# Routing of a mixture-of-experts stage: the slot arithmetic of a batch moved to the head of the next step, its four row transfers issued together

## The chip, the cores and the metric

The kernel runs on one core of a Trainium2 chip. The metric is the device time of one execution in microseconds. Five engines work side by side, each through its own instructions in a fixed order: TensorE (PE; its weight loads are shown as PEld), VectorE (DVE), ScalarE (ACT), GpSimd (POOL) and SyncE (SP, which here only issues transfers). They meet only at semaphores.

## What is computed

32 batches of 256 rows by 256 features go through two layers. The change lies in the first stage, which for each batch does the latent cross-attention of the first layer and the routing for the first feed-forward layer. Cut to what matters:

```python
x = x + tanh(g_xattn[0]) * xattn(ctx, layernorm(x), ...)     # 8 heads of 64, 376 keys
h = layernorm(x)
probs = softmax(h @ Wr + br)                    # 8 experts, for each row
topk_p, topk_e = top_k(probs, 2)
pos = (how many earlier choices of this batch took the same expert)
keep = pos < cap                                # cap = 40 rows of a batch for each expert
flat_idx = (e * B + b) * cap + min(pos, cap - 1)
buf[flat_idx] += h * keep                       # rows sent to their experts
y = relu(buf @ W1[e] + b1[e]) @ W2[e] + b2[e]   # second stage
```

The experts and the second layer follow in later stages, which the change doesn't touch.

## The kernel before

The first stage (`attend`) is a software pipeline of 35 steps, written out one after the other: step `s` begins batch `s`, does most of the attention of batches `s-1` and `s-2`, the output projection and both normalisations of batch `s-3`, and the routing of batches `s-4` and `s-5`. In every engine's `step(s, p)` the calls stand in the order in which that engine executes them; nothing else sets the order. So an instruction that waits holds up all that is written below it on its engine. `q` is `1 - p`, the other half of the double buffers.

For batch b the routing runs as follows.

- `x1_standardise` (ACT, L215) writes the normalised rows `x2h[:, p]`. It waits until the transfers that read this half two batches ago have landed (`sent[p]`), and those are the transfers of the batch whose turn came two steps before.
- `weigh` (POOL, L253) multiplies these rows by one expert's router weights, once for each of 8 experts: eight products of 128x512. `logit_part` (DVE, L259) sums each up. There are four buffers, so product e waits for the sum of product e-4. The last sum, `logit_part(7)`, and `logits_sum`, `logits_shift` and `choose(0)` to `choose(7)` (softmax, the two best experts, their one-hot rows `oh`) stand in the next step.
- `router_count` (PE, L381) counts choices with three small matmuls into the bank `a_work`, and `counts_in` (DVE, L325) takes them out of it.
- `place(0)` to `place(4)` (DVE, L335 to L355) are ten instructions on tiles of 128x4 to 128x32: the first row of each expert's region (`at_b`), two sums, the test against the capacity (`kept`, L342), the slot, the indices `sidx`, the weight (L352) and the row number (L355).
- `dispatch` (POOL, L205) issues four indirect transfers, each of which sends 128 rows of `x2h` to `slots` by a column of `sidx`. It waits for the last instruction of `place`.

The other names that the prediction uses: `row_max` (DVE, L914) takes scores out of PSUM with their row maxima and `exps` (ACT, L769) follows it; `turn_prob` (PE, L1221) transposes the exponentials and `turned_out` copies them out of PSUM, half on ACT (L777) and half on DVE (L934); `v_out` (ACT, L762) frees `a_work`; `turn_c` (PE, L1148) and `router_count` wait for it; `att_low` (DVE, L947) subtracts two tiles in SBUF; `output` (PE) is the output projection and `out_stat` (DVE, L953) its statistics; on POOL `norm1` and `norm2` turn statistics of batch `s-3` into scales, `norm0` (L181 to L190 on `a_var`, `a_nm`, `a_rs`, `a_sh`) those of batch `s`, and `residual` (L669) is an addition of 128x512.

In the kernel before, `place` of batch `s-4` stands in the second half of DVE's step, among `row_max`, `turned_out` and the first sums of the products of batch `s-3`, while GpSimd computes these products. `dispatch` of batch `s-5` is cut in two: two transfers behind `norm1`, two behind `norm2`.

Of the kernel before, what the change touches and what calls it, by code (L numbers as in the profile page):

```python
# [398 lines left out]
def attend(nc, t, keep):  # L399
# [3 lines left out]
    with ctx:  # L403
# [245 lines left out]
        def _(eng):  # L649
# [22 lines left out]
            def step(s, p):  # L672
                q = 1 - p
                if isinstance(s, int) and s == 4:
                    eng.wait_ge(zeroed, 16 * N_CLEAR)
                if here(s - 3):
                    norm1(eng, s - 3)
                if routed(s - 5):
                    dispatch(eng, s - 5, q, range(QT))
                if live(s):  # L680
                    norm0(s)
                if here(s - 3):
                    norm2(eng, s - 3)
                if routed(s - 5):
                    dispatch(eng, s - 5, q, range(QT, QT * 2))
                if live(s - 2):
                    residual(s - 2, p)
                if here(s - 3):
                    for e in range(E0):
                        weigh(eng, s - 3, q, e)  # L690
# [6 lines left out]
        def _(eng):  # L697
# [91 lines left out]
            def step(s, p):  # L789
# [15 lines left out]
                if live(s - 2):  # L805
                    k_high(s - 2, p, 3)
                    exps(s - 2, 5, 0)
                    exps(s - 2, 5, 1)
                if here(s - 4):
                    router_exp(eng, s - 4)  # L810
                if live(s - 2):
                    v_out(s - 2, p, 0)
                    turned_out(s - 2, 2, 0)
# [64 lines left out]
        def _(eng):  # L878
# [101 lines left out]
            def step(s, p):  # L980
# [17 lines left out]
                if live(s - 2):  # L998
                    turned_out(s - 2, 1, 1)
                if here(s - 4):  # L1000
                    logit_part(eng, s - 4, 7)
                if live(s - 2):
                    row_max(s - 2, p, 5, 0)
                if live(s - 3):
                    att_low(s - 3, 3)
                if here(s - 4):
                    logits_sum(eng, s - 4)
                if live(s - 2):
                    row_max(s - 2, p, 5, 1)
                if isinstance(s, int) and s == B + 2:  # L1010
                    w1_lower(1)
                if here(s - 4):
                    logits_shift(eng, s - 4)
                if live(s - 1):
                    mask_line(s - 1, q)
                if live(s - 2):
                    over_sum(s - 2, 1)
                if live(s - 1) and not (isinstance(s, int) and s == 1):
                    kvin_low(s - 1, q, 0)
                if here(s - 4):  # L1020
                    choose(eng, s - 4, 0)
                if live(s - 1) and not (isinstance(s, int) and s == 1):
                    kvin_low(s - 1, q, 1)
                if here(s - 4):
                    choose(eng, s - 4, 1)
                if live(s - 3):
                    out_stat(s - 3)
                if here(s - 4):
                    choose(eng, s - 4, 2)
                if live(s - 2):  # L1030
                    turned_out(s - 2, 2, 1)
                if here(s - 4):
                    choose(eng, s - 4, 3)
                if live(s - 3):
                    out_centre(s - 3)
                if live(s - 2):
                    row_max(s - 2, p, 6, 0)
                if here(s - 4):
                    choose(eng, s - 4, 4)
# [3 lines left out]
                if here(s - 4):  # L1043
                    choose(eng, s - 4, 5)
# [3 lines left out]
                if here(s - 4):  # L1048
                    choose(eng, s - 4, 6)
# [3 lines left out]
                if here(s - 4):  # L1053
                    choose(eng, s - 4, 7)
                if live(s - 2):
                    row_max(s - 2, p, 7, 1)
                if here(s - 3):
                    out_norm(eng, s - 3, q)
                if live(s):
# [26 lines left out]
                if routed(s - 4):  # L1086
                    place(eng, s - 4, p, 0)
                if live(s - 1):
                    row_max(s - 1, q, 2, 1)
                if routed(s - 4):  # L1090
                    place(eng, s - 4, p, 1)
# [4 lines left out]
                if routed(s - 4):  # L1096
                    place(eng, s - 4, p, 2)
# [4 lines left out]
                if routed(s - 4):  # L1102
                    place(eng, s - 4, p, 3)
# [4 lines left out]
                if routed(s - 4):  # L1108
                    place(eng, s - 4, p, 4)
# [1569 lines left out]
```

## Time and profile before

| | us |
|---|---|
| median of 3 runs | 2470.74 (2461.04 to 2481.05) |
| the profiled execution | 2471.47 |
| its span, first to last instruction | 2469.7 |
| first stage, up to about | 1393 |
| of it 26 alike steps, 142.4 to 1232.4 | 1090.0, so 41.92 for each |
| PE busy in these | 942.43 of 1090.0 |
| DVE, ACT, POOL busy in these | 851.52, 631.30, 562.00 |

The span is cut by time: the stretches are bounded by `out_stat`, which opens the second third of a step. All times of rows are of this one execution, in microseconds from its start.

### The profile page before, as it was taken

How to read it: one execution, taken by the hardware profiler on the slowest of the kernel's cores; microseconds unless marked ns; L12 is line 12 of the kernel's file. 1: busy time of each engine (PE TensorE's matmuls, PEld its weight loads, DVE VectorE, ACT ScalarE, POOL GpSimd, SP SyncE). 2: the span in 40 equal slices, each digit the busy share in tenths (PEclk: the TensorE clock that was granted, in tenths of full speed). 3: DMA queues.
4: the chain of work that ended last, by engine and by line, in shares of the span. 5: the costliest groups of instructions: out<-in, count | busy, mean ns of one | idle time of the engine just before them, and what ended most of it. 6: DMA issues, size and time to landing. Idle time of an engine off the chain costs nothing. (4 is left out here: it accounts for less than half of the span.)

```text
span 2469.7 us, 48999 instructions
## 1 busy us (share of the span) xinstructions
PE 2257.1 (91%) x15114; PEld 1860.6 (75%) x15114; DVE 1860.9 (75%) x5977; ACT 1288.7 (52%) x3220; POOL 1021.0 (41%) x1410
## 2 busy tenths in 40 slices
PE   9988888989888888888896999999998999999998
PEld 6756565656565666666664999999997888888886
DVE  5787878778787878777877755555557899899887
ACT  6655655555555565556562433333334555555553
POOL 1445555464645454545455200000025555555541
PEclk9989898999899898899897999999999999999999
DMA  5321111111111111111101422222122222122210
GB/s 202 123 70 33 46 33 38 42 35 44 36 44 35 40 39 40 33 46 41 32 28 56 146 80 91 80 78 78 45 83 58 60 71 63 61 71 63 60 52 18
DMA packets 136370, 147.71 MB, mean 60 GB/s; under 512 B 23106, under 2 KB 122681, under 8 KB 135856
## 3 DMA queue, kind: packets, MB, share of 16 engines
q1 hardware_dynamic: 122969, 123.18, 15.5%
q0 software_dynamic: 12288, 21.21, 3.0%
q8 instruction: 124, 2.03, 0.3%
q14 instruction: 134, 1.10, 0.1%
q10 hardware_dynamic: 855, 0.19, 0.1%
HBM read 102.09 MB, written 54.79 MB: 64 GB/s over the span
## 5 line engine op out<-in xcount | busy, mean ns | idle before, releaser
L769 ACT ACTIVATE a_prob<-a_prob,a_nmax 128x376 f32<-128x376 f32 x512 | 309.2, 605 | 267.3 <-DVE a_nmax L914 265.2
L914 DVE CUSTOM_DVE_ANT_0 a_prob<-a_score,a_mask_row 128x376 f32<-128x376 f32 x512 | 273.6, 541 | 59.1 <-PE a_score L1212 53.6
L1517 ACT ACTIVATE e_hidden<-e_first,keep_b 128x256 f32<-128x256 f32 x320 | 134.6, 472 | 281.2 <-PE e_first L80 279.4
L1212 PE MATMUL a_score<-a_kT,a_qT 64*128 64x376 f32 x1024 | 242.3, 585 | 27.9 <-DVE a_nmax L914 27.9
L1221 PE MATMUL a_turned<-keep_ident,a_prob 128*128 128x128 f32 (+1 forms) x1536 | 229.2, 286 | 27.7 <-DVE a_probT L934 21.0
L1221 PEld LDWEIGHTS a_turned<-keep_ident,a_prob 128*128 128x128 f32 (+1 forms) x1536 | 177.8, 144 | 91.5 <-issue 74.1
L80 PE MATMUL e_second<-e_w,e_hidden 128*128 128x256 f32 x1920 | 239.4, 284 | 0.0
L80 PEld LDWEIGHTS e_second<-e_w,e_hidden 128*128 128x128 f32 x1920 | 232.4, 191 | 0.0
L253 POOL TENSOR_TENSOR w_in<-r_x2h,keep_b 128x512 f32<-128x512 f32 x124 | 189.8, 1548 | 57.8 <-ACT r_x2h L215 38.3
L777 ACT ACTIVATE a_probT<-a_turned 128x384 f32<-128x384 f32 x256 | 124.5, 486 | 134.1 <-PE a_turned L1221 134.1
L1247 PE MATMUL a_work<-a_probT,a_vo 128*64 128x256 f32 (+1 forms) x1152 | 187.6, 473 | 3.3 <-DVE a_probT L934 2.3
L934 DVE COPY a_probT<-a_turned 128x384 f32<-128x384 f32 x256 | 139.6, 545 | 62.9 <-PE a_turned L1221 62.9
L1750 POOL COPY o_row<-keep_row 128x4 uint32<-128x4 uint32 x32 | 10.0, 311 | 410.3 <-DMA answers<-e_y 410.2
L1247 PEld LDWEIGHTS a_work<-a_probT,a_vo 128*64 128x64 f32 (+1 forms) x1152 | 91.0, 167 | 115.2 <-issue 90.4
L1212 PEld LDWEIGHTS a_score<-a_kT,a_qT 64*128 64x128 f32 x1024 | 99.2, 209 | 99.4 <-issue 76.6
L181 POOL TENSOR_SCALAR r_var<-r_mv 128x2 f32<-128x2 f32 x64 | 12.5, 195 | 370.1 <-issue 328.0
L205 POOL DMA_INDIRECT slots<-r_x2h,r_sidx x128 | 136.4, 1066 | 60.8 <-issue 46.7
L1755 POOL DMA_INDIRECT w_in<-answers,o_row x128 | 132.9, 1038 | 58.8 <-issue 31.1
L80 PE MATMUL a_work<-a_wkv,a_kvin 128*128 128x512 f32 (+1 forms) x576 | 154.2, 403 | 1.4 <-DVE a_att L942 1.4
L1564 DVE CAST e_hidden<-e_hidden 128x512 fp32r<-128x512 f32 x160 | 68.6, 429 | 95.4 <-ACT e_hidden L1517 95.4
L80 PE MATMUL e_first<-e_rowsT,e_w 128*128 128x256 f32 x960 | 118.5, 283 | 0.0
L80 PEld LDWEIGHTS a_work<-a_wkv,a_kvin 128*128 128x128 f32 (+1 forms) x576 | 101.6, 186 | 21.5 <-issue 1.7
(242 smaller groups left out, 5661.2 us busy)
## 6 DMA issues: line engine op xcount, KB each, us to landing
a_share<-shares SPq DMA_DIRECT2D x256, 64.0 KB, 2.6
w_in<-W SPq DMA_DIRECT2D x32, 512.0 KB, 4.0
slots<-a_zeros SPq DMA_DIRECT2D x8, 1280.0 KB, 8.3
keep_rows<-slots SPq DMA_DIRECT2D x40, 256.0 KB, 4.0
answers<-e_y SPq DMA_DIRECT2D x40, 256.0 KB, 2.3
a_xn<-x SPq DMA_DIRECT2D x32, 256.0 KB, 2.9
a_xr<-x SPq DMA_DIRECT2D x32, 256.0 KB, 3.2
shares<-a_rden_rows SPq DMA_DIRECT2D x512, 0.5 KB
```

Of the source, the lines that this page charges most:

```text
L80: last = nc.tensor.matmul(out, stationary(a, t), moving(b, t), start=start and n == 0, stop=stop and n == len(todo) - 1)
L205: nc.gpsimd.indirect_dma_start(out=t["slots"], out_offset=bass.IndirectOffsetOnAxis(ap=sidx[:, p, n:n + 1], axis=0), in_=x2h[:, p, n // 2] ...
L253: nc.gpsimd.tensor_tensor(weighed[e % len(weighed)], x2h[:, p], wr_rows[:, :, e].unsqueeze(1).to_broadcast([P, QT, D]), ALU.mult).then_inc ...
L769: nc.scalar.activation(prob[:, u % 4, a], prob[:, u % 4, a], ACT.Exp, bias=nmax[:, u % 4, a:a + 1], scale=-1.0, accum_out=den[:, u % 4, a: ...
L777: nc.scalar.activation(probT[:, u // 2 % 2, a, :, u % 2 * P:(u % 2 + 1) * P], turned_keys[a], ACT.Copy) \
L914: nc.vector.tensor_tensor_reduce(prob[:, u % 4, a], score[SCORE_AT[u][a]][:, 0:NKV], mask_row[:, p], -1.0, 3.0e38, ALU.add, ALU.min, nmax[ ...
L934: nc.vector.tensor_copy(probT[:, u // 2 % 2, a, :, u % 2 * P:(u % 2 + 1) * P], turned_keys[a]) \
L1212: nc.tensor.matmul(score[SCORE_AT[u][a]][:, 0:NKV], qT[rows, p, m, i * P:(i + 1) * P], kT[rows, p, m], start=True, stop=True).then_inc(sco ...
L1221: last = nc.tensor.transpose(turned_keys[a][0:hi - lo, j], prob[:, u % 4, a, lo:hi], ident[:])
L1247: last = nc.tensor.matmul(out[64 * a:64 * a + 64, 0:S], vo[0:hi - lo, p, j, m, a], probT[0:hi - lo, m % 2, a, j], start=j == 0, stop=j == 2)
L1517: nc.scalar.activation(hidden[:, 2 * j + i], first[:, j, i * CH:(i + 1) * CH], ACT.Relu, bias=b1[:, 2 * j + i, bass.ds(e, 1)]).then_inc(re ...
L1755: nc.gpsimd.indirect_dma_start(out=picked[p][:, n], out_offset=None, in_=t["answers"][0:rows], in_offset=bass.IndirectOffsetOnAxis(ap=row[ ...
```

## The change

`place` leaves the second half of the step in which the batch was counted and goes to the head of the next one, behind `logit_part(7)`, `row_max` and `att_low`, its parts put between `row_max`, `mask_line`, `over_sum` and `kvin_low`. `logits_sum`, `logits_shift` and `choose` each move a few places down. `router_exp` on ACT moves behind `v_out(0)` and `turned_out(2)`. `dispatch` issues its four transfers together, behind `norm1` and ahead of `norm0`. No instruction is added or removed.

```diff
                 if here(s - 3):
                     norm1(eng, s - 3)
                 if routed(s - 5):
-                    dispatch(eng, s - 5, q, range(QT))
+                    dispatch(eng, s - 5, q)
                 if live(s):
                     norm0(s)
                 if here(s - 3):
                     norm2(eng, s - 3)
-                if routed(s - 5):
-                    dispatch(eng, s - 5, q, range(QT, QT * 2))
                 if live(s - 2):
                     residual(s - 2, p)
                 if here(s - 3):
@@ -806,11 +804,11 @@
                     k_high(s - 2, p, 3)
                     exps(s - 2, 5, 0)
                     exps(s - 2, 5, 1)
+                    v_out(s - 2, p, 0)
+                    turned_out(s - 2, 2, 0)
                 if here(s - 4):
                     router_exp(eng, s - 4)
                 if live(s - 2):
-                    v_out(s - 2, p, 0)
-                    turned_out(s - 2, 2, 0)
                     exps(s - 2, 6, 0)
                     exps(s - 2, 6, 1)
                     turned_out(s - 2, 3, 0)
@@ -997,65 +995,74 @@
                     attended(s - 3, 3)
                 if live(s - 2):
                     turned_out(s - 2, 1, 1)
+                    row_max(s - 2, p, 5, 0)
                 if here(s - 4):
                     logit_part(eng, s - 4, 7)
-                if live(s - 2):
-                    row_max(s - 2, p, 5, 0)
                 if live(s - 3):
                     att_low(s - 3, 3)
+                if routed(s - 5):
+                    place(eng, s - 5, q, 0)
+                if live(s - 2):
+                    row_max(s - 2, p, 5, 1)
+                if routed(s - 5):
+                    place(eng, s - 5, q, 1)
+                if isinstance(s, int) and s == B + 2:
+                    w1_lower(1)
+                if live(s - 1):
+                    mask_line(s - 1, q)
+                if routed(s - 5):
+                    place(eng, s - 5, q, 2)
+                if live(s - 2):
+                    over_sum(s - 2, 1)
+                if routed(s - 5):
+                    place(eng, s - 5, q, 3)
+                if live(s - 1) and not (isinstance(s, int) and s == 1):
+                    kvin_low(s - 1, q, 0)
+                if routed(s - 5):
+                    place(eng, s - 5, q, 4)
                 if here(s - 4):
                     logits_sum(eng, s - 4)
-                if live(s - 2):
-                    row_max(s - 2, p, 5, 1)
-                if isinstance(s, int) and s == B + 2:
-                    w1_lower(1)
-                if here(s - 4):
-                    logits_shift(eng, s - 4)
-                if live(s - 1):
-                    mask_line(s - 1, q)
-                if live(s - 2):
-                    over_sum(s - 2, 1)
-                if live(s - 1) and not (isinstance(s, int) and s == 1):
-                    kvin_low(s - 1, q, 0)
-                if here(s - 4):
-                    choose(eng, s - 4, 0)
                 if live(s - 1) and not (isinstance(s, int) and s == 1):
                     kvin_low(s - 1, q, 1)
                 if here(s - 4):
-                    choose(eng, s - 4, 1)
+                    logits_shift(eng, s - 4)
                 if live(s - 3):
                     out_stat(s - 3)
+                if live(s - 2):
+                    turned_out(s - 2, 2, 1)
+                if here(s - 4):
+                    choose(eng, s - 4, 0)
+                if live(s - 3):
+                    out_centre(s - 3)
+                if here(s - 4):
+                    choose(eng, s - 4, 1)
+                if live(s - 2):
+                    row_max(s - 2, p, 6, 0)
                 if here(s - 4):
                     choose(eng, s - 4, 2)
-                if live(s - 2):
-                    turned_out(s - 2, 2, 1)
-                if here(s - 4):
-                    choose(eng, s - 4, 3)
-                if live(s - 3):
-                    out_centre(s - 3)
-                if live(s - 2):
-                    row_max(s - 2, p, 6, 0)
-                if here(s - 4):
-                    choose(eng, s - 4, 4)
                 if live(s - 2):
                     row_max(s - 2, p, 6, 1)
                     over_sum(s - 2, 2)
                 if here(s - 4):
-                    choose(eng, s - 4, 5)
+                    choose(eng, s - 4, 3)
                 if live(s - 2):
                     attended(s - 2, 0)
                     turned_out(s - 2, 3, 1)
                 if here(s - 4):
-                    choose(eng, s - 4, 6)
+                    choose(eng, s - 4, 4)
                 if live(s - 2):
                     row_max(s - 2, p, 7, 0)
                     att_low(s - 2, 0)
                 if here(s - 4):
-                    choose(eng, s - 4, 7)
+                    choose(eng, s - 4, 5)
                 if live(s - 2):
                     row_max(s - 2, p, 7, 1)
+                if here(s - 4):
+                    choose(eng, s - 4, 6)
                 if here(s - 3):
                     out_norm(eng, s - 3, q)
+                if here(s - 4):
+                    choose(eng, s - 4, 7)
                 if live(s):
                     stat(s, p)
                 if live(s - 2):
@@ -1083,30 +1090,20 @@
                     w1_lower(0)
                 if live(s - 1):
                     row_max(s - 1, q, 2, 0)
-                if routed(s - 4):
-                    place(eng, s - 4, p, 0)
                 if live(s - 1):
                     row_max(s - 1, q, 2, 1)
-                if routed(s - 4):
-                    place(eng, s - 4, p, 1)
                 if live(s - 2):
                     attended(s - 2, 2)
                 if here(s - 3):
                     logit_part(eng, s - 3, 0)
-                if routed(s - 4):
-                    place(eng, s - 4, p, 2)
                 if live(s - 2):
                     turned_out(s - 2, 7, 1)
                 if here(s - 3):
                     logit_part(eng, s - 3, 1)
-                if routed(s - 4):
-                    place(eng, s - 4, p, 3)
                 if live(s - 1):
                     row_max(s - 1, q, 3, 0)
                 if here(s - 3):
                     logit_part(eng, s - 3, 2)
-                if routed(s - 4):
-                    place(eng, s - 4, p, 4)
                 if live(s - 2):
                     att_low(s - 2, 2)
                 if here(s - 3):
```

On VectorE, in the second half of the first step that has a `place`: before, behind the first of the sums (`r_lgr`), the parts of `place` (`r_kept` to `keep_row`) stand among copies, sums and row maxima (ISA).

```order
L342 TENSOR_SCALAR r_kept<-r_pos 128x4
L343 SCALAR_TENSOR_TENSOR r_slot<-r_pos,r_base 128x4
L934 COPY a_probT<-a_turned1 128x3x128
L259 TENSOR_REDUCE r_lgr<-w2_in 128x2
L346 TENSOR_SCALAR r_slot_s<-r_kept 128x4
L348 TENSOR_TENSOR r_wsel<-r_top,r_kept 128x4
L914 ISA a_prob,a_nmax<-a_score2,a_mask_row 128x376
L914 ISA a_nmax 128x1
L259 TENSOR_REDUCE r_lgr<-r_rT 128x2
L350 TENSOR_TENSOR r_sidx<-r_slot,r_slot_s 128x4
L352 TENSOR_SCALAR keep_weight<-r_wsel,r_tgate 128x4
L355 CAST keep_row<-r_slot 128x4
```

In the changed kernel the same stretch of VectorE holds only the copies, sums and row maxima.

```order
L932 COPY a_probT<-a_turned1 128x3x128
L259 TENSOR_REDUCE r_lgr<-w2_in 128x2
L912 ISA a_prob,a_nmax<-a_score2,a_mask_row 128x376
L912 ISA a_nmax 128x1
L259 TENSOR_REDUCE r_lgr<-r_rT 128x2
L945 TENSOR_TENSOR a_att2<-a_att,a_att2 128x256
```

Ten instructions have left it, and `att_low` (`a_att2`) now follows straight on a sum. They stand on VectorE at the head of the next step:

```order
L342 TENSOR_SCALAR r_kept<-r_pos 128x4
L343 SCALAR_TENSOR_TENSOR r_slot<-r_pos,r_base 128x4
L923 RECIPROCAL a_rden<-a_den 128x2x2
L926 STREAM_TRANSPOSE a_rden_rows<-a_rden 128x32
L346 TENSOR_SCALAR r_slot_s<-r_kept 128x4
L348 TENSOR_TENSOR r_wsel<-r_top,r_kept 128x4
L893 TENSOR_TENSOR a_kvin2<-a_kvin,a_kvin2 128x2x256
L350 TENSOR_TENSOR r_sidx<-r_slot,r_slot_s 128x4
L352 TENSOR_SCALAR keep_weight<-r_wsel,r_tgate 128x4
L355 CAST keep_row<-r_slot 128x4
L264 TENSOR_TENSOR r_lg<-r_lgr,r_br 128x16
L893 TENSOR_TENSOR a_kvin2<-a_kvin,a_kvin2 128x2x120
```

All ten now stand behind the last sum of the products and ahead of `out_stat`. On GpSimd, before, a step from `norm1` (`r_rs1`) to the addition `residual` (`r_xb`):

```order
L187 TENSOR_TENSOR r_rs1<-r_var1,r_minus_half 128x2
L205 DMA slots<-r_x2h,r_sidx 10240x256 x2
L181 TENSOR_SCALAR a_var<-a_mv 128x2
L184 TENSOR_SCALAR a_nm<-a_mv 128x2
L181 TENSOR_SCALAR a_var<-a_mv 120x1
L184 TENSOR_SCALAR a_nm<-a_mv 120x1
L187 TENSOR_TENSOR a_rs<-a_var,r_minus_half 128x3
L190 TENSOR_TENSOR a_sh<-a_nm,a_rs 128x3
L181 TENSOR_SCALAR r_var2<-r_mv2 128x2
...
L190 TENSOR_TENSOR r_sh2<-r_nm2,r_rs2 128x2
L205 DMA slots<-r_x2h,r_sidx 10240x256 x2
L669 TENSOR_TENSOR r_xb<-a_xr,a_bo 128x512
```

and in the changed kernel:

```order
L187 TENSOR_TENSOR r_rs1<-r_var1,r_minus_half 128x2
L205 DMA slots<-r_x2h,r_sidx 10240x256 x4
L181 TENSOR_SCALAR a_var<-a_mv 128x2
L184 TENSOR_SCALAR a_nm<-a_mv 128x2
L181 TENSOR_SCALAR a_var<-a_mv 120x1
```

The two later transfers have joined the first two, ahead of `norm0`; the addition now follows on `norm2` (`r_sh2`).

## Rows read from the trace of the kernel before

**Rows 1.** Busy time by stretch: PE, PEld, DVE, ACT, POOL; PE's clock; DMA share, GB/s.
```profile
69.30:102.40 33.10, 32.50 (x226) 24.53 (x225) 26.86 (x90) 23.97 (x65) 17.57 (x21) 1.00 0.22 79
102.40:142.40 40.00, 35.58 (x229) 26.11 (x229) 33.31 (x112) 24.36 (x65) 17.74 (x21) 0.91 0.35 115
142.40:1232.40 1090.00, 942.43 (x5904) 677.87 (x5903) 851.52 (x2912) 631.30 (x1690) 562.00 (x650) 0.91 0.13 39
```
**Rows 2.** Waits of PE, 400 to 1200 us: total, times, longest.
```profile
PE a_work L381 <- ACT a_vo L762: 41.1, 19, 2.6
PE a_work L1148 <- ACT a_vo L762: 36.0, 19, 2.8
```
**Rows 3.** Timeline of one step: start, duration, engine, operation [idle before, releaser].
```profile
796.93 1.72 POOL L253 TENSOR_TENSOR a_weighed<-r_x2h,keep_b 128x512 f32<-128x512 f32 x1
797.13 3.03 DVE L342 TENSOR_SCALAR r_kept<-r_pos 128x4 f32<-128x4 f32 x1
798.53 1.60 POOL L253 TENSOR_TENSOR w_in<-r_x2h,keep_b 128x512 f32<-128x512 f32 x1
...
800.83 0.52 PE L1221 MATMUL a_turned<-keep_ident,a_prob 128*128 128x128 f32 x3 [1.68 <-DVE a_probT L934]
...
802.82 1.56 DVE L352 TENSOR_SCALAR keep_weight<-r_wsel,r_tgate 128x4 f32<-128x4 f32 x1
...
803.25 0.63 PE L1148 MATMUL a_work<-keep_ident,a_xh 120*128 120x120 f32 x2 [1.90 <-ACT a_vo L762]
...
803.81 1.63 PE L1212 MATMUL a_score<-a_kT,a_qT 64*128 64x376 f32 x4
```
**Rows 4.** Instructions of `place` by line, 300 to 1250 us: ns min/median/max.
```profile
L335 DVE TENSOR_TENSOR r_at_b<-r_oh,r_slot x22: 185/860/868, 331.7 to 1211.7; 128x32 f32<-128x32 f32 x22
L342 DVE TENSOR_SCALAR r_kept<-r_pos x22: 157/1484/3026, 334.2 to 1214.1; 128x4 f32<-128x4 f32 x22
L352 DVE TENSOR_SCALAR keep_weight<-r_wsel,r_tgate x22: 216/1560/1566, 338.5 to 1219.7; 128x4 f32<-128x4 f32 x22
```
**Rows 5.** One microsecond of the next step, columns as in the first group.
```profile
844.00:845.00 1.00, 0.00 (x0) 0.00 (x0) 1.00 (x3) 1.00 (x4) 1.00 (x2) 0.50 0.00 0
```
**Rows 6.** Timeline, norms and transfers of that step.
```profile
825.23 0.19 POOL L181 TENSOR_SCALAR a_var<-a_mv 128x2 f32<-128x2 f32 x1 [4.04 <-issue]
...
831.07 1.12 POOL L205 DMA_INDIRECT slots<-r_x2h,r_sidx  x1 [0.30 <-issue]
...
833.44 1.09 ACT L215 ACTIVATE r_x2h<-r_x,r_sh,r_rs 128x256 f32<-128x256 f32 x2 [2.99 <-DMA slots<-r_x2h,r_sidx]
...
835.07 0.23 PE L381 MATMUL a_work<-r_ohs,r_tri 128*128 128x8 bf16 x3 [2.05 <-ACT a_vo L762]
```
**Rows 7.** The transfers of `dispatch` by line: ns min/median/max.
```profile
L205 POOL DMA_INDIRECT slots<-r_x2h,r_sidx x128: 967/1070/2046, 145.4 to 1392.1; - x128
```
**Rows 8.** Timeline, PE and DVE in steps 3 and 4, products without `place`.
```profile
83.10 1.63 PE L80 MATMUL a_work<-a_wkv,a_kvin 128*120 128x512 f32 x6
...
92.43 0.45 DVE L947 TENSOR_TENSOR a_att<-a_att 128x256 fp32r<-128x256 f32 x1
...
93.28 0.40 PE L1148 MATMUL a_work<-keep_ident,a_xh 120*128 120x120 f32 x2 [0.60 <-ACT a_vo L762]
93.60 1.53 PE L1212 MATMUL a_score<-a_kT,a_qT 64*128 64x376 f32 x8
...
116.25 1.63 PE L80 MATMUL a_work<-a_wkv,a_kvin 128*120 128x512 f32 x6
```
**Rows 9.** Timeline, `out_stat` in the step of Rows 3.
```profile
816.29 0.76 DVE L953 BATCH_NORM_STATS2 a_stats<-keep_bank 128x6 f32<-128x256 f32 x2 [0.86 <-PE keep_bank L80]
```
**Rows 10.** Timeline, `residual` and `att_low` in step 32, and the last steps.
```profile
1289.56 1.31 POOL L669 TENSOR_TENSOR r_xb<-a_xr,a_bo 128x512 f32<-128x512 f32 x1
1290.33 0.83 DVE L947 TENSOR_TENSOR a_att<-a_att 128x256 fp32r<-128x256 f32 x1
...
1336.28 1.09 ACT L215 ACTIVATE r_x2h<-r_x,r_sh,r_rs 128x256 f32<-128x256 f32 x2 [5.74 <-DMA slots<-r_x2h,r_sidx]
```

More of the change, by code:

```diff
@@ L1024, in step @@
                 if here(s - 4):
-                    choose(eng, s - 4, 1)
+                    logits_shift(eng, s - 4)
                 if live(s - 3):
                     out_stat(s - 3)
-                if here(s - 4):
-                    choose(eng, s - 4, 2)
                 if live(s - 2):
@@ L1038, in step @@
                 if here(s - 4):
-                    choose(eng, s - 4, 4)
+                    choose(eng, s - 4, 2)
                 if live(s - 2):
```

## The prediction

> **What bounds the kernel now.** I read the busy times by stretch first. In 26 alike steps of the first stage PE is busy for 942.43 of 1090.0 us, DVE for 851.52, and PE's mean granted clock is 0.91 [rows 1]. So PE is nearest to the bound, yet it loses (1090.0 - 942.43)/26 = 5.7 us in each step of 41.92 us, and some of its busy time is at the low clock. The stretch ahead of them is the one to compare with: from 69.3 to 102.4 us the eight products run but nothing is placed or sent, and it takes 33.10 us with PE busy for 32.50 of it at clock 1.00. The next, with the first placing, takes 40.00 at 0.91 [rows 1].
>
> The waits of PE say where. In 19 steps it waited 41.1 us at `router_count` and 36.0 us at `turn_c`, both for `v_out` on ACT: 2.16 and 1.90 us a step [rows 2]. The timeline gives each a cause.
>
> At `turn_c` it is placing. The test against the capacity (L342), an instruction on 128x4, took 3.03 us and ended with the second of two products on GpSimd (798.53 + 1.60 = 800.13) [rows 3]. By line the same instructions take 0.157 to 3.026 us (L342), 0.216 to 1.566 (L352), 0.185 to 0.868 (L335) [rows 4]. So they are held while a product of 1.5 us runs. Behind them on DVE stand `turned_out`, for which PE then waited 1.68 us, and `row_max`, for which `exps` and behind it `v_out` waited, so PE another 1.90 [rows 3]. Then the clock falls: at 844 us, in the next step's like gap, PE does nothing and the granted clock is 0.50, the 1.2 GHz level [rows 5]. A step's mean of 0.91 is (1 - 0.91)/0.5 x 41.92 = 7.5 us at it. The two matmul groups of one `scores` then take 1.63 us [rows 3], where two calls took 1.53 at full clock [rows 8].
>
> At `router_count` it is the transfers. ACT was idle 2.99 us until the last of them had landed, because they stand behind `norm2`; PE waited 2.05 for the `v_out` behind it [rows 6].
>
> **The change, part by part.** The base is a step in which neither cause is there, products, attention, choosing and norms all running: from `project_v(2)` of step 3 at 83.10 to that of step 4 at 116.25, 33.15 us [rows 8].
>
> Placing leaves the products. `logit_part(7)`, which waits for the last product, stands ahead of it, and the next work on GpSimd is `norm1`, which waits for `out_stat`, behind it. So all ten instructions should take their lowest, 0.15 to 0.22 us by [rows 4]: 1.6 us together. It is not free. It stands ahead of `out_stat`, where DVE was idle 0.86 us for PE's output projection [rows 9], and two small instructions of `choose` (some 0.15 each, as the shortest of `place` are) have moved behind `out_stat`. 1.6 - 0.86 - 0.3 leaves 0.44 us on the path, through `out_stat` and `out_centre`, for which `project_q` waits. Bounds: 0, if matmuls in flight cover it, and 1.6, if the idle time goes elsewhere. I take 0.44.
>
> The transfers. Two more now stand between `norm1` and `norm0`. A transfer and the gap behind it are 1.07 + 0.30 us by [rows 6, 7], so 2.7 us more, and GpSimd was idle 4.04 us there [rows 6]: hidden, with 1.3 us left. Their indices are ready ahead of `norm1`. Behind `norm2` 2.7 us go, and `residual` moves up. ACT no longer waits, since the last transfer then lands ahead of `norm2`; what ends last there is `att_high` on ACT itself. The products start some 3 us sooner, so there is no loss on that side. The shortest transfer is 0.967 us, the longest 2.046 [rows 7]; four at the longest are 4 x 2.35 = 9.4 us, less the two that stood there before (2.7) 6.7, which outlasts the 4.04 us by 2.6. This is a rival.
>
> `router_count` itself was not in step 3: 0.23 us on PE [rows 6], I take 0.2. The move of `router_exp` costs 0: ACT has 631.30 busy of 1090.0 [rows 1], and the result is wanted behind `out_stat`.
>
> New blocking. DVE and GpSimd now run side by side without placing to line them up, and `att_low(2)` subtracts two SBUF tiles in the middle of the products. With the addition `residual` running it took 0.83 us and not 0.45: it ended with what was left of the addition and then its own [rows 8, 10]. In step 3 it got in just ahead of a product (0.45) [rows 8]. In the changed kernel it comes some tenths later against the products, whose start also moves by tenths. Bounds: 0 and one product, 1.5; I take 0.7, the middle, since nothing fixes the phase. Behind it stands `row_max(3,1)`, for which PE's `scores(5)` waits, so it is on the path.
>
> The Trainium skill, "SBUF — State Buffer", section Who interferes with whom, says that a VectorE instruction with two SBUF inputs, or a copy or tensor_scalar in a two-port mode, blocks fully against a GpSimd instruction that reads SBUF. The trace agrees for placing (3.03 us for 128x4) [rows 3]; it speaks against this change for `att_low`, which the 0.7 stands for. The same page holds that a transfer issued by GpSimd can be starved of descriptors by VectorE's copies. Of 128 transfers here the longest took 2.046 us [rows 7], so no run here shows more than a doubling; the rival of the long transfers is that rule in this kernel.
>
> The sum. A step is 33.15 + 0.44 + 0.2 + 0.7 = 34.5 us against 41.92: 7.42 less. Steps 5 to 32 are 28: 208 us. Step 4, 40.00 before [rows 1], places nothing any more: about 33.5, so 6.5. In step 33 ACT waited 5.74 us for the transfers [rows 10], which goes, but the last placing and its four transfers now stand in the last step, behind its last product, and bound the stage: 3 us net. Together 217.5. The stages behind are unchanged. 2471.47 - 217.5 = 2254 us for the profiled execution, which stands 0.7 above the median, well inside its spread.
>
> A check from the other side: 2.16 + 1.90 + 1.68 of waits, and up to 7.5/2 = 3.7 for work at half clock, are 9.4; 41.92 - 33.15 is 8.8.
>
> **Rivals.**
>
> A. The blocking moves. `att_low(2)` is held by two products, 3.0 us as L342 was [rows 3], and PE idles there. The step is 33.15 + 0.44 + 0.2 + 3.0 = 36.8, 5.1 less: 143 + 9.5, so 2319 us. For it: the median of L342, 1.484, is a hold of one product, and its longest one of two [rows 4]. Against: `att_low(2)` was never long in a step without placing.
>
> B. The clock. PE's waits shrink, but something still lets the clock fall in each step. Then half of the work in 7.5 us stays, 3.7: 34.5 + 3.7 = 38.2, 3.7 less, so 2471 - 104 - 9.5 = 2358 us. Against: in step 3, with a wait of 0.60 at `turn_c`, it stayed at 1.00 [rows 1, 8].
>
> C. Long transfers. `norm0` comes 2.6 us late, of which a microsecond or so is covered in ACT's queue ahead of `v_out`; 1.5 more a step: 36.0, so 2471 - 166 - 9.5 = 2296 us.
>
> D. The other side, slower. Placing is held at its new place as long as now, some 5.3 us (0.86 + 1.48 + 1.56 [rows 4] and seven more of 0.2), because GpSimd still reads SBUF there. Then 5.3 - 0.86 - 0.3 = 4.1 us stand ahead of `out_stat` uncovered, PE waits for them in one piece, the clock falls (3.7), `att_low` costs its full 1.5: 33.15 + 0.2 + 4.1 + 3.7 + 1.5 = 42.7, 0.8 more than now, so 2471 + 22 = 2493 us. It decides from the point at which the last product ends behind `row_max(5,0)`; in the order, `logit_part(7)` forbids that.
>
> E. It doesn't do what it says: the instructions are out of the products' way but DVE is the late engine at each point, so that a step stays at 41 to 42 us: 2460. Against it, DVE is busy 26.86 of 33.10 us without placing [rows 1], and the 1.6 of placing fit beside it.
>
> **How the numbers follow.** Forecast 0.60 (with its own bounds, steps of 33.3 to 35.4: 2221 to 2280), A 0.15, B 0.08, C 0.12, D 0.03, E 0.02. The forecast's low end is 33.15 + 0.2, with nothing uncovered: 8.6 x 28 + 9.5 = 250, so 2221, and I go to 2215 for the last steps. The high end takes in A and C, and stops short of most of B: 2325. A measurement of this kernel can tell about 1% from no change. Faster by over 1%: all but D and E, 0.95; same 0.02; slower 0.03.
>
> **What the profile would show.** L342, L352 and L335 at 0.15 to 0.22 us each; if not, the first step of this is wrong. ACT's wait at L215 for transfers gone, and PE's waits at L381 and at L1145 (now `turn_c`) under 0.6 us a step. Mean clock of the alike steps above 0.97; at 0.91 it is B. The maximum and median of `att_low` (now L945): a median above 0.45 is A or the 0.7. A gap ahead of `out_stat` (now L951) gone, and PE waiting there instead for some tenths. `norm0` starting on its statistics, not on the transfers. The forecast fails if a new wait on DVE stands in each step that step 3 didn't have, since every microsecond of a step counts 28 times.

## The result, and the profile after

The changed kernel takes 2272.22 us (median of 4 runs, 2267.9 to 2273.48) against 2475.89 of the kernel before beside it: a ratio of 0.9182, 95% interval 0.9134 to 0.9229, so 8.2% faster. The profiled execution took 2272.51 us, its span is 2270.7.

The busy times by stretch, bounded at `out_stat` as in [rows 1]; columns: length, PE, PEld, DVE, ACT, POOL, PE's granted clock, DMA share, GB/s:

```profile
69.00:106.00 37.00, 33.84 (x223) 24.84 (x222) 29.77 (x88) 23.85 (x64) 17.39 (x21) 0.95 0.24 82
106.00:143.40 37.40, 34.30 (x229) 25.37 (x228) 31.46 (x112) 24.00 (x65) 17.41 (x21) 0.95 0.32 101
143.40:1081.00 937.60, 896.68 (x6132) 674.29 (x6132) 800.79 (x3025) 648.81 (x1755) 582.45 (x675) 0.99 0.16 47
```

The last row is 27 steps, 5 to 31: 34.7 us each against 41.92, PE busy for 96% of them and at clock 0.99. The first two rows are steps 3 and 4, and step 3 has become longer: 37.4 us (from `out_stat` to `out_stat`) and not 33.1.

The instructions of `place` in all their 32 executions answer to [rows 4] (columns: count: ns min/median/max, first and last start):

```profile
L335 DVE TENSOR_TENSOR r_at_b<-r_oh,r_slot x32: 181/184/192, 140.4 to 1183.5; 128x32 f32<-128x32 f32 x32
L342 DVE TENSOR_SCALAR r_kept<-r_pos x32: 159/162/171, 141.2 to 1184.0; 128x4 f32<-128x4 f32 x32
L352 DVE TENSOR_SCALAR keep_weight<-r_wsel,r_tgate x32: 221/224/230, 142.5 to 1184.6; 128x4 f32<-128x4 f32 x32
```

None is held any more. The waits of PE between 400 and 1100 us, in place of [rows 2] (total, times, longest; these are all of them):

```profile
PE a_score L1209 <- DVE a_nmax L912: 18.4, 11, 2.5
PE a_work L1145 <- ACT a_vo L760: 12.2, 20, 0.6
```

The wait at `router_count` is gone, that at `turn_c` (now L1145) has shrunk from 1.90 to 0.61 us a step. A wait of up to 2.5 us at `scores` stands in 11 of 20 steps. From the timeline of a step, what answers to [rows 6, 9]:

```profile
804.29 0.76 DVE L951 BATCH_NORM_STATS2 a_stats<-keep_bank 128x6 f32<-128x256 f32 x2 [0.32 <-PE keep_bank L80]
...
813.52 0.19 POOL L181 TENSOR_SCALAR a_var<-a_mv 128x2 f32<-128x2 f32 x1 [1.84 <-issue]
...
818.22 1.08 ACT L215 ACTIVATE r_x2h<-r_x,r_sh,r_rs 128x256 f32<-128x256 f32 x2
```

Although placing now stands ahead of `out_stat`, DVE still comes there 0.32 us before PE's output is ready. GpSimd, with all four transfers done, is still idle 1.84 us before `norm0`. ACT waits for nothing at `x1_standardise`.

Where the new wait comes from is in the timeline of a longer step, rows of POOL (products), of DVE (`att_low`, L945, and a sum, L259) and of PE (`scores`):

```profile
441.99 3.11 POOL L253 TENSOR_TENSOR w_in<-r_x2h,keep_b 128x512 f32<-128x512 f32 x2
...
443.49 3.38 DVE L945 TENSOR_TENSOR a_att<-a_att 128x256 fp32r<-128x256 f32 x1
...
445.03 1.55 POOL L253 TENSOR_TENSOR r_rT<-r_x2h,keep_b 128x512 f32<-128x512 f32 x1
446.79 0.67 DVE L259 TENSOR_REDUCE r_lgr<-a_weighed 128x2 f32<-128x512 f32 x1
447.54 1.52 POOL L253 TENSOR_TENSOR a_weighed<-r_x2h,keep_b 128x512 f32<-128x512 f32 x1 [0.96 <-DVE r_lgr L259]
...
448.07 1.62 PE L1209 MATMUL a_score<-a_kT,a_qT 64*128 64x376 f32 x4 [2.51 <-DVE a_nmax L912]
```

`att_low(2)` was issued at 443.49, 0.14 us before the first of these products ended, and was done at 446.87, when the products had stopped at 446.58: the last of them waits for a sum that stands behind `att_low` on DVE. In between lies another boundary, at 445.03 to 445.11, and DVE didn't get in there. The second of the two products by itself:

```profile
443.55 1.56 POOL L253 TENSOR_TENSOR w_in<-r_x2h,keep_b 128x512 f32<-128x512 f32 x1
```

In another step DVE came at such a boundary, too, 0.08 us before a product ended, and `att_low` took its 0.41 us:

```profile
199.67 3.29 POOL L253 TENSOR_TENSOR w_in<-r_x2h,keep_b 128x512 f32<-128x512 f32 x2
201.16 0.41 DVE L945 TENSOR_TENSOR a_att<-a_att 128x256 fp32r<-128x256 f32 x1
```

In a third it was issued 0.10 us before the end of a product, missed that boundary and got in at the next:

```profile
165.06 3.06 POOL L253 TENSOR_TENSOR w_in<-r_x2h,keep_b 128x512 f32<-128x512 f32 x2
166.55 1.86 DVE L945 TENSOR_TENSOR a_att<-a_att 128x256 fp32r<-128x256 f32 x1
168.07 1.71 POOL L253 TENSOR_TENSOR r_rT<-r_x2h,keep_b 128x512 f32<-128x512 f32 x1
```

In the 27 alike steps it took 0.4 us in 12, about 1.85 in 9 and 3.33 or 3.38 in 6. In all of them it was issued 0.06 to 0.15 us before a product ended, so this distance doesn't tell the three cases apart: issued at 0.10 it took 0.42, 1.86 or 3.33 us, by step. Steps without a hold take 33.2 us, those with the longest 37.3 to 37.5: such a hold costs 4.2 us and not only its 3.0, and in each of these steps PE's mean clock is 0.95, where it is 1.00 in the steps without a hold.

### The profile page after: what moved, and what is told of

Its sections match the earlier page's. It is cut to its first block and busy times, and to the rows that moved or that the text cites. A ratio compares the mean times of both kernels' runs of the same rounds, so it can differ in the third digit from the quotient of the medians.

```text
span 2270.7 us, 48998 instructions
## 1 busy us (share of the span) xinstructions
PE 2175.3 (96%) x15114; PEld 1829.2 (81%) x15114; DVE 1772.5 (78%) x5977; ACT 1279.1 (56%) x3220; POOL 1016.9 (45%) x1410
## 5 line engine op out<-in xcount | busy, mean ns | idle before, releaser
L1209 PE MATMUL a_score<-a_kT,a_qT 64*128 64x376 f32 x1024 | 206.8, 517 | 31.2 <-DVE a_nmax L912 31.2
L1218 PE MATMUL a_turned<-keep_ident,a_prob 128*128 128x128 f32 (+1 forms) x1536 | 218.2, 278 | 1.5 <-ACT a_probT L775 1.4
L1218 PEld LDWEIGHTS a_turned<-keep_ident,a_prob 128*128 128x128 f32 (+1 forms) x1536 | 171.6, 140 | 55.2 <-issue 38.6
L253 POOL TENSOR_TENSOR w_in<-r_x2h,keep_b 128x512 f32<-128x512 f32 x124 | 194.7, 1596 | 26.8 <-ACT r_x2h L215 26.8
L1209 PEld LDWEIGHTS a_score<-a_kT,a_qT 64*128 64x128 f32 x1024 | 88.6, 188 | 87.6 <-issue 60.4
L1244 PE MATMUL a_work<-a_probT,a_vo 128*64 128x256 f32 (+1 forms) x1152 | 157.2, 411 | 2.0 <-DVE a_probT L932 0.9
L205 POOL DMA_INDIRECT slots<-r_x2h,r_sidx x128 | 130.4, 1019 | 55.3 <-issue 41.0
L1244 PEld LDWEIGHTS a_work<-a_probT,a_vo 128*64 128x64 f32 (+1 forms) x1152 | 79.5, 145 | 88.7 <-issue 46.7
```

The lines of the kernel that those rows point to most:

```text
L205: nc.gpsimd.indirect_dma_start(out=t["slots"], out_offset=bass.IndirectOffsetOnAxis(ap=sidx[:, p, n:n + 1], axis=0), in_=x2h[:, p, n // 2] ...
L253: nc.gpsimd.tensor_tensor(weighed[e % len(weighed)], x2h[:, p], wr_rows[:, :, e].unsqueeze(1).to_broadcast([P, QT, D]), ALU.mult).then_inc ...
L1209: nc.tensor.matmul(score[SCORE_AT[u][a]][:, 0:NKV], qT[rows, p, m, i * P:(i + 1) * P], kT[rows, p, m], start=True, stop=True).then_inc(sco ...
L1218: last = nc.tensor.transpose(turned_keys[a][0:hi - lo, j], prob[:, u % 4, a, lo:hi], ident[:])
L1244: last = nc.tensor.matmul(out[64 * a:64 * a + 64, 0:S], vo[0:hi - lo, p, j, m, a], probT[0:hi - lo, m % 2, a, j], start=j == 0, stop=j == 2)
```

## The experiments

"Step" is the mean of steps 5 to 31, (start of `out_stat` in step 32 - start in step 5)/27, from each run's timeline. Each median is of 4 runs, those of e10 and e11 of 2. For the changed kernel it is (1081.34 - 143.85)/27 = 34.72. Before, it is (1275.76 - 142.86)/27 = 41.96.

| run | what it is | median us | ratio to before, interval | step us |
|---|---|---|---|---|
| changed kernel | both parts | 2272.22 | 0.9182 (0.9134 to 0.9229) | 34.72 |
| e1_place_only | placing moved, transfers split | 2357.18 | 0.9525 (0.9504 to 0.9547) | 37.96 |
| e2_dispatch_only | transfers together, placing not moved | 2371.75 | 0.9588 (0.9565 to 0.9611) | 38.45 |
| e3_low_late | changed, `att_low(2)` at the head of the next step | 2223.43 | 0.8983 (0.8966 to 0.9) | 33.35 |
| e4_filler | before, with filler matmuls | 2434.79 | 0.9839 (0.9822 to 0.9856) | 40.46 |
| e5_halves | changed, products in halves | 2335.7 | 0.9444 (0.9406 to 0.9482) | 36.93 |
| e6_low_late_split | e3, transfers split | 2342.45 | 0.9465 (0.9431 to 0.9499) | 37.64 |
| e7_place_old | e3, placing among the products | 2373.92 | 0.9588 (0.9553 to 0.9624) | 38.66 |
| e8_max_first | e3, a row maximum ahead of a sum | 2220.18 | 0.8971 (0.8939 to 0.9003) | 33.21 |
| e9_low_first | e8, `att_low` ahead of a row maximum | 2205.67 | 0.8906 (0.8879 to 0.8933) | 32.74 |
| e10_behind_sum3 | changed, `att_low(2)` one sum later | 2313.81 | 0.9342 (0.9305 to 0.9379) | 36.29 |
| e11_ahead_sum2 | changed, `att_low(2)` one sum sooner | 2248.95 | 0.908 (0.9045 to 0.9116) | 34.16 |

**The two parts one at a time.** The first two runs undo one part each.

```diff
 # e1: on the changed kernel, GpSimd
                 if routed(s - 5):
-                    dispatch(eng, s - 5, q)
+                    dispatch(eng, s - 5, q, range(QT))
...
                     norm2(eng, s - 3)
+                if routed(s - 5):
+                    dispatch(eng, s - 5, q, range(QT, QT * 2))
 # e2: on the kernel before, the reverse of this
```

> The changed kernel with the transfers split again: two behind norm1, two behind norm2. My theory (two causes, each with its own wait): placing is out of the products, so its instructions stay at 0.15 to 0.22 us and the clock stays up, but ACT waits about 3 us for the last two transfers and PE about 2 us behind it, so a step of 35.5 to 37 us against 34.7 in the changed kernel: 2300 to 2335 us. Rival (the transfers were hidden anyway): 2272 us as the changed kernel.

> The kernel before with all four transfers behind norm1, placing where it was. My theory: ACT's wait at x1_standardise goes (2.99 us) and PE's 2.16 us at router_count with it, but the instructions of place stay held by products (L342 median about 1.5 us), PE still waits at turn_c and the clock still falls: 28 steps of about 2 us less, 2400 to 2430 us. Rival (all is one chain and the transfers were its head): near 2272 us. Rival (placing alone counts): 2470 us.

Both parts count, and neither rival holds. But e1 is slower than I expected and e2 faster. In e1 PE waits 42.1 us in 17 steps at `router_count`, 2.48 a step, and `att_low(2)` is held in every step (1.1 to 1.5 us, once 4.1): the products begin later against DVE's queue, so the phase differs. In e2 L342 isn't held any more (median 153 ns, where I expected 1.5 us), but L335 is (columns as for `place` above):

```profile
L335 DVE TENSOR_TENSOR r_at_b<-r_oh,r_slot x32: 181/1597/1618, 125.9 to 1285.4; 128x32 f32<-128x32 f32 x32
L342 DVE TENSOR_SCALAR r_kept<-r_pos x32: 149/153/303, 129.0 to 1286.0; 128x4 f32<-128x4 f32 x32
```

Which instruction is held is a matter of phase, that is, of where DVE's instructions fall against the boundaries of the products; all ten together take 5.7 us a step in e2 as in the kernel before, and 1.7 in the changed one. For clean prices `att_low` has to leave the products first.

**`att_low` away from the products.**

```diff
 # e3: on the changed kernel, VectorE
-                if live(s - 2):
-                    att_low(s - 2, 2)
...
                 if live(s - 3):
+                    att_low(s - 3, 2)
                     att_low(s - 3, 3)
```

> The changed kernel with att_low(2) moved from among the products to the head of the next step, right ahead of att_low(3), where no product runs. My theory (what is left above the undisturbed step is att_low(2) held by one or two products, in 15 of 27 steps): no att_low above 0.9 us, all steps at 33.2 to 33.6 us, clock of the alike steps 1.00, so 1.2 to 1.5 us a step less and about 4 us in each of the first two: 2220 to 2235 us. Rival (the hold moves on to another instruction, or att_low ahead of the output projection costs as much as it saves): 2265 to 2280 us.

As expected, to a tenth of a microsecond a step. Every one of the 27 steps now takes 33.3 or 33.4 us. PE waits only 0.6 us at `turn_c`. The busy times of a long stretch (columns as before):

```profile
142.00:1050.00 908.00, 890.21 (x6185) 675.31 (x6184) 774.91 (x3042) 647.32 (x1770) 581.81 (x682) 1.00 0.16 48
```

So the changed kernel loses 34.72 - 33.35 = 1.4 us a step to this hold, and some 4 us in steps 3 and 4 each.

**The parts again, without that hold.**

```diff
 # e6: e3 with the transfers split as in e1
 # e7: e3 with the parts of place, logits_sum, logits_shift and choose
 #     on VectorE and router_exp on ScalarE where they were before
 #     (and row_max(5,0) behind logit_part(7) again)
```

> The kernel with att_low(2) at the head of the next step (steps of 33.35 us, 2223 us), and the transfers split again, two behind norm2: the transfers alone, without holds. Theory: ACT waits 2.9 to 3.4 us for the last transfer and PE 2.1 to 2.5 us at router_count, nothing else changes, so a step of 35.4 to 35.9 us: 2280 to 2297 us. Rival (the price was in the holds that came with the shift of the products): within 15 us of 2223.

> The same kernel (att_low(2) at the head of the next step, four transfers together) with placing back among the products and the choosing where it was before: placing alone. Theory: the ten instructions are held as in the kernel before, PE waits 2 to 4 us at turn_c and scores and the clock falls to half behind it: a step of 37.5 to 38.7 us, 2345 to 2380 us. Rival (att_low was the instruction that made PE wait, and placing only stood beside it): 2225 to 2260 us.

Placing costs 38.66 - 33.35 = 5.3 us a step, as expected. The moves of the choosing, of `router_exp` and of `row_max(5,0)` are in this price, and no run tells them apart from it; but the ten instructions of `place` alone take 5.95 us a step here against 1.67 in e3. The transfers alone cost 37.64 - 33.35 = 4.3, twice what I expected; the wait itself was as expected, 42.1 us in 17 steps, 2.48 a step. The rest is the clock. PE's timeline of e6 behind the wait, in order `router_count`, `scores`, `times_v`:

```profile
832.76 0.23 PE L381 MATMUL a_work<-r_ohs,r_tri 128*128 128x8 bf16 x3 [2.35 <-ACT a_vo L762]
832.97 2.54 PE L1210 MATMUL a_score<-a_kT,a_qT 64*128 64x376 f32 x8
835.44 2.15 PE L1245 MATMUL a_work<-a_probT,a_vo 128*64 128x256 f32 x12
```

The eight records of `scores` take 1.53 us at full clock [rows 8] and `times_v` 1.52; here they take 1.0 and 0.6 us more, behind a wait of 2.35 us. The mean clock between 142 and 1050 us:

```profile
142.00:1050.00 908.00, 833.24 (x5481) 614.53 (x5481) 690.94 (x2706) 576.62 (x1569) 516.13 (x605) 0.95 0.15 44
```

PE's busy time in a step is 833.24/908 x 37.64 = 34.5 us, against 890.21/908 x 33.35 = 32.7 in e3, with the same work: 1.8 us, and 1.8 + 2.5 = 4.3. The same term is why e2 was faster than I expected: with the transfers together the clock of the alike steps rose from 0.91 to 0.95 and PE's busy time fell from 36.2 to 34.7 us a step. The two prices add up to 9.6; both causes together are 41.96 - 33.35 = 8.6 (in the alike steps of the kernel before `att_low(2)` was never held, 0.41 us in each). So they overlap by a microsecond.

**The clock alone.**

```diff
 # e4: on the kernel before, TensorE, steps 4 and on
+                        for a in range(2):
+                            eng.wait_ge(nmax_ok[a], NG * (s - 1) + 3)
+                        keep_busy(nc, score[0][:, 0:P], ident[:], ident[:], 8)
                     turn_c(s)
```

> The kernel before with 8 matmuls of 128x128 more in each step, ahead of turn_c, on a score bank that is free by then; they fill about 1.8 us of the gap in which PE waits for v_out and compute nothing that is used. Theory of the clock (PE's idle time there drops the clock to half and that costs a few us a step): granted clock of the alike steps above 0.97, scores and times_v behind it at their full-clock durations, 2 to 3.7 us a step less: 2370 to 2420 us. Rival (the clock is a symptom, the holds on DVE set the step): 2465 to 2500 us.

Here L342 is still held (median 1477 ns) and PE still waits at `router_count`, but the clock between 142 and 1050 us is up:

```profile
142.00:1050.00 908.00, 803.19 (x5485) 604.77 (x5484) 738.05 (x2532) 541.17 (x1457) 484.33 (x567) 0.98 0.14 42
```

It gives back 41.96 - 40.46 = 1.5 us a step, 1.6% of the time: more than the rival allows, less than I had put on it. In this run `scores` and `times_v` behind `router_count` are slow in some steps (2.50 and 2.19 us), so the low clock went only in part. PE's busy time in a step is 803.19/908 x 40.46 = 35.8 us, of it 1.95 for the filler, so 33.8 for the work that took 942.43/26 = 36.2 before: 2.4 us less. About one of these went into longer waits, half of it at `scores` (0.85 us a step before, 1.39 here). So 1.5 us is what this filler gave back, and not all that the low clock costs.

**What ends a hold.** Three runs on `att_low(2)` among the products of the changed kernel.

```diff
 # e5: each product in two instructions
+        for k in range(QT):
+            last = nc.gpsimd.tensor_tensor(weighed[e % len(weighed)][:, k], x2h[:, p, k], wr_rows[:, :, e], ALU.mult)
+            if k == QT - 1:
+                last.then_inc(weighed_ok, 1)
 # e10: att_low(2) behind logit_part(3); e11: att_low(2) ahead of logit_part(2)
```

> The changed kernel with each of the eight products issued as two of 128x256, the same work. Theory of the lock (att_low waits until the GpSimd instruction in flight ends, sometimes until the next one has ended too): the longest att_low falls from 3.4 us to about 2 us, the holds of one instruction from 1.86 to 1.2 or less, so about half of the 1.5 us that they cost a step: 2245 to 2262 us. Rival (the hold follows from the data or from the whole product, for instance from the tile and not from the instruction): holds of 1.86 and 3.4 us as before, 2270 to 2280 us.

> The changed kernel with att_low(2) behind logit_part(3) and not ahead of it. Theory (once GpSimd has got ahead, att_low is held until GpSimd itself has nothing to run, which is when a product waits for a sum that stands behind att_low; the sum of product 3 lets product 7 run): the longest hold grows by about a product less the 0.6 us of the sum, to 4.2 to 4.4 us. Rival (att_low waits for the two instructions in flight at most): longest 3.4 us or less.

> The changed kernel with att_low(2) ahead of logit_part(2) and not behind it. Theory (a hold lasts until GpSimd runs out of products, and product 6 now waits for a sum behind att_low): the longest hold falls to 2.4 to 2.7 us. Rival (two instructions in flight at most): 3.4 us or nearly, by phase.

The first went against what I expected: with instructions of half the length the longest hold grew to 4.40 us, and the kernel is 2.8% slower than the changed one. The timeline of a hold in e5 (L254 is a product, L261 a sum, L947 `att_low`):

```profile
168.89 3.27 POOL L254 TENSOR_TENSOR w_in<-r_x2h,keep_b 128x256 f32<-128x256 f32 x4
...
169.73 4.33 DVE L947 TENSOR_TENSOR a_att<-a_att 128x256 fp32r<-128x256 f32 x1
172.13 1.65 POOL L254 TENSOR_TENSOR r_rT<-r_x2h,keep_b 128x256 f32<-128x256 f32 x2
...
174.74 1.66 POOL L254 TENSOR_TENSOR a_weighed<-r_x2h,keep_b 128x256 f32<-128x256 f32 x2 [0.96 <-DVE r_lgr L261]
```

Five or six instructions of GpSimd run in that time, up to 173.78, and DVE gets in at none of their boundaries; it ends at 174.06, when the products have stopped for want of a sum. The hold is longer because `att_low` was issued 4.05 us before the products stopped, where it was 3.09 in the changed kernel (446.58 - 443.49): two halves take 1.66 us and a whole product 1.55, and `att_low` comes a third of a product sooner against them. Such long holds came in 17 of 27 steps, in the changed kernel in 6. The other two runs move the point at which they stop, and the longest `att_low` follows it (e10, then e11; ns min/median/max):

```profile
L945 DVE TENSOR_TENSOR a_att<-a_att x128: 411/421/4303, 40.4 to 1187.0; 128x256 fp32r<-128x256 f32 x128
```

```profile
L945 DVE TENSOR_TENSOR a_att<-a_att x128: 411/421/2545, 40.8 to 1123.7; 128x256 fp32r<-128x256 f32 x128
```

4.30 and 2.55 us, as the theory had it, around the 3.43 of the changed kernel. That two instructions in flight bound the hold doesn't stand. In these three runs `att_low(2)` is issued 0.66 us or more before the end of a GpSimd instruction, and its times in the 27 steps fall in two groups with nothing between them: 1.05 to 1.08 (10 steps) and 4.30 to 4.37 us (17) in e5, 1.24 to 1.30 (14) and 4.21 to 4.26 (13) in e10, 0.94 to 1.02 (20) and 2.45 to 2.49 (7) in e11. So it got in at the first boundary, or at none until GpSimd's queue stopped.

**What bounds the rest.**

```diff
 # e8: on e3, VectorE
-    logit_part(eng, s - 3, 1)
     row_max(s - 1, q, 3, 0)
+    logit_part(eng, s - 3, 1)
 # e9: on e8, VectorE at the head of the step
-    row_max(s - 2, p, 5, 0)
     logit_part(eng, s - 4, 7)
     att_low(s - 3, 2)
     att_low(s - 3, 3)
+    row_max(s - 2, p, 5, 0)
```

> The kernel with att_low(2) at the head of the next step, and row_max(3,0) ahead of logit_part(1) and not behind it. PE's last wait in a step is 0.6 us at turn_c for v_out, which stands on ACT behind the exponential of this row maximum. Theory (PE is the bound now and every wait of PE counts): the 0.6 us goes, a step of 32.8 us: 2204 to 2212 us. Rival (something else ends last there, for instance the sum that comes later holds up a product, or PE's work is the bound already): 2219 to 2226 us.

> The kernel with row_max(3,0) ahead of logit_part(1), and at the head of the step logit_part(7) and the two att_low ahead of row_max(5,0). PE's last wait there is 0.44 us at the output projection for att_low. Theory (it waits for it because three instructions stand ahead): the wait goes, 32.8 to 32.9 us a step, 2207 to 2213 us. Rival (PE's own work is the bound, or row_max(5,0) later costs as much): 2217 to 2223 us.

e8 came out as the rival had it: the 0.6 us at `turn_c` went, but PE then waited 0.44 us at the output projection for `att_low` (8.4 us in 19 steps), and a step lost only 0.14. e9 took that wait away too: 32.74 us a step and 2205.67 us, just below what was expected. It is the fastest run here, and PE hardly idles:

```profile
142.00:1050.00 908.00, 906.92 (x6285) 685.23 (x6285) 786.20 (x3089) 661.39 (x1799) 594.16 (x689) 1.00 0.16 49
```

## Why the prediction was right, point by point

2254 us was forecast with a range of 2215 to 2325; 2272 was measured. In the profiled executions 199.0 us went (2471.47 - 2272.51) where I had 217.5.

- **Placing leaves its holds**: right, all ten instructions at 0.13 to 0.23 us, 1.7 together. e7 prices it at 5.3 us a step without the transfers' wait.
- **0.44 us for it on the path, 0.2 for `router_count`**: too high. A step without a hold takes 33.2 us (e.g. 211.68 - 178.50), as the base of 33.15 did, and DVE still waits 0.32 us at `out_stat`. Both terms measured nothing.
- **The transfers hidden ahead of `norm0`**: right, with 1.84 us left where I worked out 1.3. ACT's and PE's waits went. Rival C did not occur: the four transfers took their 0.97 to 1.07 us. What I had not seen is that their price holds a clock term: e6 has 1.8 us of half clock behind a wait of 2.35 us.
- **0.7 us for `att_low`, bounds 0 and one product**: the mechanism was right, the size wrong. It costs 34.72 - 33.2 = 1.5 us a step. What failed is "Bounds: 0 and one product, 1.5": a hold can last until GpSimd has no instruction to run, up to 3.4 us here, and e5, e10 and e11 set it to 4.4, 4.3 and 2.5. Rival A had the 3.0 us, but for every step; it came in 6 of 27, where it cost 4.2 with the clock, and a shorter one in 9 more. That "nothing fixes the phase" holds only in part: DVE came to the same boundary in every step, and what was open is whether it got in.
- **The sum of a step**: 34.5 against 34.72, since the two errors nearly cancel: 0.6 us too much, 0.8 too little. A step came out right by that luck, 7.24 us less where I had 7.42.
- **Steps 3 and 4**: I had 0 and 6.5 us less. From `out_stat` of step 3 to that of step 5 it was 73.1 us before and is 74.8 now: both steps have a hold of 3.4 us. That is 8 of the missing 18 us, and another 5 are the 27 steps (0.18 each). All from `out_stat` of step 32 on gave 4.5 us, where I had 10.4 (7.4 for step 32 and 3). In the last step `output` waits 8.61 us for `att_low`, and its four transfers end at 1156.66 us, behind `out_stat` (1153.89). Behind this last `out_stat` the span is 4.5 us longer than before (1116.8 against 1112.3); 1.5 of it is the second stage's later start, and the rest comes in small pieces far behind it, in stages that are the same in both kernels; its cause stays open.
- **The clock**: right in direction (0.91 to 0.99), and about right in size: PE was busy for 36.2 us a step before and for 32.7 in e3, 3.5 us for the same work, near the 3.7 of my check from the other side. Of this e4's filler alone gave back no more than its 1.5 us net. The check itself closed by luck: it put the 1.68 us of one wait for `turned_out` on every step, where PE waited 12.8 us in 9 of 19 steps, and left out what it waited at `scores`. Waits of PE in the kernel before, 400 to 1200 us, the two that [rows 2] doesn't have:

```profile
PE a_score L1212 <- DVE a_nmax L914: 16.9, 19, 1.4
PE a_turned L1221 <- DVE a_probT L934: 12.8, 9, 1.7
```

- **B, D and E** did not occur; a lower clock (0.95) was left in 8 of the 27 steps only, all with a hold.

The measured ratio is one number for both parts, with the new hold in it. e1 and e2 save 118 and 104 us, together more than the 204 of both. That doesn't mean that one part does the other's work: in the changed kernel the hold of `att_low(2)` takes some 49 us back (e3). Without it the sum is the other way round, 134 us (e6) and 103 (e7) against 252 (e3), so while one of the causes is still there, taking away the other gives less.

## What to carry to other kernels

Where VectorE and GpSimd run side by side, list VectorE's instructions with two SBUF inputs or plain SBUF copies and tensor_scalar forms that fall among long GpSimd instructions (here subtractions, the tests and weights of `place` and a cast); put them where GpSimd waits anyway, whatever their size, and don't bound the cost by one GpSimd instruction. If GpSimd's queue waits for VectorE, the hold ends at the latest where this wait begins, so the order of the two decides its length. And price a wait of TensorE with the clock behind it: here 2.5 us of waiting cost 4.3.

## What the runs showed of the hardware

- VectorE and GpSimd meet not only at semaphores. A VectorE subtraction of 128x256 with both inputs in SBUF took 0.41 to 0.42 us with no product or addition on GpSimd beside it, and up to 4.40 beside the products. Issued inside a GpSimd instruction, it always waited for the end of that one, and then got in at once or, in 17 of 27 steps of e5, 13 of e10 and 7 of e11, only when GpSimd's queue stopped. What decides that was not found.
- The smallest instructions paid the same: a test on 128x4 took 0.16 to 3.03 us in the kernel before. The sums of the products (one input, 128x512) took 0.67 to 0.68 us beside a product as without one.
- GpSimd's indirect transfers did not hold VectorE: `att_low(0)` at 809.85 us took 0.42 us while one was being issued, and so did the other 26 of the changed kernel's alike steps (0.416 to 0.422).
- Two products of 128x256 took 1.65 to 1.68 us, one of 128x512 1.51 to 1.56 by most rows.
- TensorE's granted clock fell behind waits of 2 to 3 us, and the length of the wait alone didn't decide it. At `router_count` in the kernel before PE waited 2.0 to 2.8 us in each of the 27 steps, and `scores` behind it was slower than its 1.53 us in 10 of them: 2.88 us behind a wait of 2.06, but 1.53 behind one of 2.61. In e6 it was slower in 26 of 27, behind waits of 2.25 to 3.3 us.

The Trainium skill, "SBUF — State Buffer", section Who interferes with whom, has the rule that the second to issue blocks fully until the first has finished. The trace agrees on the blocking, and that the sums, with one input, are not blocked; on its length the measurement decides: it lasted over five or six GpSimd instructions in a row (e5).
